# Placing edges by source in one fp16 pass, the basis mix dealt over three stages, slot writes begun earlier

## What is computed

```python
edge_index = jnp.stack([src, dst])
# first layer: a message per edge, summed by source
x_ij = jnp.concatenate([x[src], x[dst]], axis=1)
out = jax.ops.segment_sum(relu(x_ij @ W.T + b), src, num_segments=1250)
# last layer: two relations, 30 bases of 512 x 512 each, for each of two inner layers
w = jnp.einsum('rb,bio->rio', att, basis)
```

## Time and profile before

| what | us |
|---|---|
| median of 3 runs | 1941.36 (1940.92 to 1942.94) |
| span of the profiled execution, first to last instruction | 1934.6 |
| first block of the sort, and loading before it | up to 90.0 |
| second block of the sort | 90.0 to 137.85 |
| bucket stage | 137.85 to 185.06 |
| placing and unpacking | 185.06 to 293.35 |
| counting | 293.35 to 455.20 |

### The profile page before, as it was taken

One profiled execution on the slowest core, in us unless ns is written; L12 is line 12 of the kernel. 1 busy time (PEld: TensorE's weight loads), 2 busy tenths in 40 slices (PEclk: granted clock), 3 DMA queues, 4 the chain that ended last, 5 costly groups with the idle time before them and its releaser, 6 DMA issues. The chain is left out here.

```text
span 1934.6 us, 27686 instructions
## 1 busy us (share of the span) xinstructions
PE 1608.4 (83%) x7565; PEld 981.3 (51%) x7566; DVE 1167.7 (60%) x2310; ACT 471.2 (24%) x884; POOL 705.2 (36%) x605
## 2 busy tenths in 40 slices
PE   6755956776498999998888459998498899999998
PEld 6751633335443555554555435554246545874486
DVE  5779958884365777775467766665774832113222
ACT  4301103432212555554344210000110111001100
POOL 0001877887094776660000347775330010000000
PEclk9997988998698999999899569999799999999999
DMA  0017844005802766682388337776104201430033
GB/s 25 0 47 285 275 136 120 1 1 172 306 27 92 210 197 187 187 169 45 126 317 331 101 100 211 210 209 171 27 1 144 96 1 72 155 122 1 0 136 135
DMA packets 76346, 248.96 MB, mean 129 GB/s; under 512 B 14901, under 2 KB 28582, under 8 KB 68346
## 3 DMA queue, kind: packets, MB, share of 16 engines
q1 hardware_dynamic: 38618, 147.08, 21.1%
q0 software_dynamic: 34592, 96.87, 18.9%
q10 hardware_dynamic: 3072, 4.20, 0.7%
HBM read 215.93 MB, written 32.00 MB: 128 GB/s over the span
## 5 line engine op out<-in xcount | busy, mean ns | idle before, releaser
L664 POOL DMA_INDIRECT tab_slots<-slot_words,slot_address x160 | 238.1, 1488 | 244.5 <-issue 233.3
L693 POOL DMA_INDIRECT e_rows<-tab_h,idx_h x176 | 178.6, 1015 | 293.4 <-POOLq L50 219.8
L1443 PE MATMUL dense_pY<-weights,dense_xT_block 128*128 128x512 f32 x640 | 284.3, 602 | 0.0
L1491 PE MATMUL dense_pY<-parts,dense_number 128*128 128x512 f32 x1000 | 237.7, 399 | 7.1 <-DMA dense_number<-tab_edges_to 7.1
L994 POOL DMA_INDIRECT e_rows<-tab_q,idx_q x192 | 182.0, 948 | 99.4 <-issue 38.9
L1491 PEld LDWEIGHTS dense_pY<-parts,dense_number 128*128 128x128 f32 x1000 | 188.7, 189 | 54.8 <-DMA dense_number<-tab_edges_to 8.6
L787 PE MATMUL e_pS<-e_rows,e_onehot_ring 128*128 128x512 f32 x352 | 194.2, 643 | 22.1 <-DVE e_rows L763 19.2
L1443 PEld LDWEIGHTS dense_pY<-weights,dense_xT_block 128*128 128x128 f32 x640 | 121.9, 194 | 143.1 <-issue 143.1
L1067 PE MATMUL e_pS<-e_rows,e_onehot_f 128*128 128x512 f32 x384 | 181.4, 596 | 0.0
L877 PE MATMUL count_pA<-count_onehot_d,count_onehot_s 128*128 128x512 f16 (+1 forms) x576 | 117.4, 352 | 63.8 <-DVE count_onehot_d L855 60.3
L763 DVE TENSOR_TENSOR e_rows<-e_rows,e_pW 128x1024 f32<-128x1024 f32 x88 | 107.3, 1220 | 69.3 <-DMA e_rows<-tab_h,idx_h 69.0
(11 more groups left out here) (312 smaller groups left out, 2448.4 us busy)
## 6 DMA issues: line engine op xcount, KB each, us to landing
basis_piece<-in_L_gnn_basis_pieces SPq DMA_DIRECT2D x32, 2048.0 KB, 7.9
dense_number<-tab_edges_from SPq DMA_DIRECT2D x20, 1280.0 KB, 5.4
tab_edges_from<-counts_turned SPq DMA_DIRECT2D x10, 1280.0 KB
tab_edges_to<-counts_total SPq DMA_DIRECT2D x10, 640.0 KB
dense_number<-tab_edges_to SPq DMA_DIRECT2D x10, 640.0 KB, 4.6
tab_w<-basis_wout ACTq DMA_DIRECT2D x128, 32.0 KB
weights<-tab_w SPq DMA_DIRECT2D x4, 1024.0 KB, 6.3
weights<-in_L_gnn_W_T SPq DMA_DIRECT2D x3, 1024.0 KB
```

Of the source, the lines that this page charges most:

```text
L664: pool.indirect_dma_start(self.table, bass.IndirectOffsetOnAxis(self.address[:, t:t + 1], 0), self.words[:, t, :], None).then_inc(self.pla ...
L693: pool.indirect_dma_start(self.rows[:, q, s, :], None, self.table, bass.IndirectOffsetOnAxis(self.idx[:, j * 2 + s:j * 2 + s + 1], 0)).the ...
L1443: ins = self.nc.tensor.matmul(self.banks.at(g), self.xt[:, b % 2, c, :], weights[:, c, :], start=c == 0, stop=c == 3)
L1491: ins = self.nc.tensor.matmul(self.banks.at(self.first + b), self.number[:, b % 2, r * NB + k, :], self.parts[r][n][:, k, :], start=k == 0 ...
```

## The change

**Placing.** The packed word goes. For each tile DVE builds `onp` for that tile alone (128 columns) and two `ons` halves of 192 columns, one with the source within its block, one with the target; all three are single-source operations with fp16 input (two iotas, converted once) and fp16 output. PE makes one fp16 matmul of 384 columns per tile. At the end three DVE operations on PSUM write `loc`, `dst` and `idx_q`; the unpacking block is gone. The loops are written out.

**Basis.** The first basis' 16 pieces are dealt 6, 6, 4: six to the sort (two loaded in its first block, the rest and all the mixing in its second), six to the bucket stage as before, four to the placing. Pieces and results lie in the space of `X` and the weights, which are now one tile. The sort's rank lookup is written out for it.

**Slot writes.** 24 in the bucket stage, 36 in placing, 86 in counting, 14 beside storing the counts (before: 0, 56, 88, 16).

```diff
-WITH_BUCKETS = 6
+WITH_SORT, WITH_BUCKETS = 6, 12
...
+    def load_some(self, eng, first, last):
+        if first == 0:
+            eng.dma_start(self.mix[:, :], self.mix_in).then_inc(self.mixed, 16)
+        for n in range(first, last):
+            wait(eng, self.used, (n - 1) * 2)
+            eng.dma_start(self.piece[:, n % 2, :], self.pieces[(n + self.first) * P:(n + self.first + 1) * P, :]
+                          ).then_inc(self.loaded[n % 2], 16)
...
+        basis.allocate(ctx, stage_semaphores(nc, ctx, f"{name}_basis"))
...
+            def _(sp):
+                basis.load_some(sp, 0, 2)
...
+            def _(sp):
+                basis.load_some(sp, 2, basis.steps * 2)
+
+            @block.scalar
+            def _(act):
+                for n in range(basis.steps * 4):
+                    basis.store(act, n // 4, n // 2 % 2, n % 2)
+                basis.end_store(act)
...
+                basis.start_multiply(pe)
+                for n in range(4):
+                    basis.multiply(pe, n // 4, n // 2 % 2, n % 2)
                 pe.wait_ge(prefix_ready, 1)
...
+                for g in range(T // GT):
+                    w = g % 2
+                    wait(pe, taken, g - 1)
+                    for u in range(GT):
+                        t = g * GT + u
+                        ins = nc.tensor.matmul(pg[:, w, u, :, :].rearrange("p n l -> p (n l)"), onehotT[0:HI, t, :],
+                                               pre[:, :, :, t].rearrange("p n l -> p (n l)"), start=True, stop=True)
+                    ins.then_inc(gathered, 1)
+                    if g >= 2:
+                        n = g + 2
+                        basis.multiply(pe, n // 4, n // 2 % 2, n % 2)
...
+        @block.gpsimd
+        def _(pool):
+            table.place(pool, 0, PLACED_WITH_BUCKETS)
...
-            for f, factor in packed:
-                link(nc.vector.scalar_tensor_tensor(value, f, float(factor), value, ALU.mult, ALU.add))
...
+            nc.vector.tensor_copy(iota_p[:, :], C.f("iota_p", EP))
+            nc.vector.tensor_copy(iota_s[:, :], C.f("iota_slot", EP)[:, 0:slots]).then_inc(iota_ready, 1)
+            v.wait_ge(iota_ready, 1)
+            for t in range(T):
+                wait(v, placed, t + 1 - RING)
+                nc.vector.tensor_scalar(onp[:, t % RING, :], iota_p[:, :], pos_p[:, t:t + 1], None, ALU.is_equal)
+                for n in range(2):
+                    ins = nc.vector.tensor_scalar(ons[:, t % RING, n, :], iota_s[:, :], pos_s[:, t:t + 1],
+                                                  values[n][:, t:t + 1], ALU.is_equal, ALU.mult)
+                ins.then_inc(built, 1)
             v.wait_ge(placed, T)
-            nc.vector.tensor_copy(sorted_out, po[:, 0:slots])
+            nc.vector.tensor_scalar(loc, po[:, 0, :], 1.0, None, ALU.subtract)
+            nc.vector.tensor_copy(other, po[:, 1, :])
+            nc.vector.tensor_copy(other_index, po[:, 1, :])
...
+            for t in range(T):
+                pe.wait_ge(built, t + 1)
+                nc.tensor.matmul(po[:, :, :].rearrange("p n s -> p (n s)"), onp[:, t % RING, :],
+                                 ons[:, t % RING, :, :].rearrange("p n s -> p (n s)"),
+                                 start=t == 0, stop=t == T - 1).then_inc(placed, 1)
+                if t == 0:
+                    basis.start_multiply(pe)
+                if t % mixed_after == mixed_after - 1:
+                    n = t // mixed_after
+                    basis.multiply(pe, n // 4, n // 2 % 2, n % 2)
...
-PLACED_WHILE_PLACING, PLACED_WHILE_COUNTING = 56, 144
+PLACED_WITH_BUCKETS, PLACED_WHILE_PLACING, PLACED_WHILE_COUNTING = 24, 60, 146
```

More of the change, by code:

```diff
@@ L173, with __init__, banks, allocate @@
     PIECES = D * D // BCH // BW
-    def __init__(self, nc, name, pieces, mix, wtab, first, last):
+    def __init__(self, nc, name, pieces, mix, wtab, first, last, space=None):
         self.nc, self.name = nc, name
         self.pieces, self.mix_in, self.dst = pieces, mix, wtab
-        self.first, self.steps = first, (last - first) // 2
+        self.first, self.steps, self.space = first, (last - first) // 2, space
     def begin(self, ctx, sem):
+        self.allocate(ctx, sem)
+        self.banks(ctx)
+    def banks(self, ctx):
+        self.ps = ctx.enter_context(self.nc.psum_tensor(f"{self.name}_ps", [P, 4, D], F32))
+    def allocate(self, ctx, sem):
         nc = self.nc
@@ L445, in _, with bucket_edges @@
                                  ).then_inc(summed, 1)
+                basis.start_multiply(pe)
+                for n in range(4):
+                    basis.multiply(pe, n // 4, n // 2 % 2, n % 2)
                 pe.wait_ge(prefix_ready, 1)
[L448 to L462, removed]
+                for g in range(T // GT):
[9 more added lines that the diff above has]
+                        basis.multiply(pe, n // 4, n // 2 % 2, n % 2)
+def bucket_edges(nc, name, C, key, rel, pair_block, tile_bucket, tile_bank, bucket_end, pos_p, pos_s, value, basis,
+                 table):
     with ExitStack() as ctx:
@@ L605, in _ @@
         def _(act):
-            def step(i):
-                for n in range(4):
-                    basis.store(act, i, n // 2, n % 2)
-            peeled(act, basis.steps, step)
+            for n in range(basis.steps * 4):
+                basis.store(act, n // 4, n // 2 % 2, n % 2)
             basis.end_store(act)
@@ L628, in _ @@
             v.wait_ge(placed, T)
-            nc.vector.tensor_copy(sorted_out, po[:, 0:slots])
+            nc.vector.tensor_scalar(loc, po[:, 0, :], 1.0, None, ALU.subtract)
+            nc.vector.tensor_copy(other, po[:, 1, :])
+            nc.vector.tensor_copy(other_index, po[:, 1, :])
         @block.tensor
         def _(pe):
-            def step(i, first=False, last=False):
-                for u in range(STEP):
-                    pe.wait_ge(built, i * STEP + (u + 1))
-                    nc.tensor.matmul(po[:, 0:slots], onp[:, u // TOGETHER % BATCHES, u % TOGETHER, :], ons[:, u % RING, :],
-                                     start=first and u == 0, stop=last and u == STEP - 1).then_inc(placed, 1)
-                    if u % QUARTER == QUARTER - 1:
-                        n = u // QUARTER
-                        if first and n == 0:
-                            basis.start_multiply(pe)
-                        basis.multiply(pe, i, n // 2, n % 2)
@@ L643, in _ @@
-            step(0, first=True)
-            with pe.Fori(1, T // STEP - 1) as i:
-                step(i)
-            step(T // STEP - 1, last=True)
+            for t in range(T):
[8 more added lines that the diff above has]
+                    basis.multiply(pe, n // 4, n // 2 % 2, n % 2)
```

84 lines of the change are left out of this document (35 added, 49 removed).

## The result

The changed kernel takes **1966.35 us** (median of four, 1965.86 to 1970.09) against 1941.14 us: a ratio of 1.0144, 95% interval 1.0127 to 1.0161, so it is 1.4% slower. The forecast was 1956 us, range 1940 to 1976, slower. Sign and range held; the size was 10 us short. Every execution takes 1.7 to 1.9 us more than its span, so the profile of the kernel before (span 1934.6) is of an execution of some 1936.4 us, the fastest of its four; of the 6.8 us that were put down to what lies around the first and the last instruction, 5 are spread between executions. The profile of the changed kernel is of its slowest (1970.09 us, span 1968.2). So the spans differ by 33.6 us where the medians differ by 25.2.

What follows compares the result with a forecast made beforehand. The prediction took POOL's slot writes to bound the placing and DVE the counting. Sort +0.5, bucket stage +8.0, placing +6.2 and counting -0.4 made +14.3 us, hence 1956 us, range 1940 to 1976.

Steps and rivals of the forecast that it cites:

- What bounds the kernel now: Old stages: POOL's 56 slot writes bound the placing, PE and DVE having 15 us to spare; DVE bounds the counting.
- The placing's price: Placing: DVE bounds it at 0.62 us per tile, 114.5 us in all against 108.3, so +6.2 us.
- Break-even: Placing: the cost per tile, 0.53 us, from which rival 1's faster kernel is decided.
- The bucket stage: Bucket stage: POOL's 24 new slot writes wait for DVE's long operations and end the stage, +8.0 us.
- the danger: Bucket stage: the forecast would be wrong if DVE's chain itself grew behind POOL's writes; no size given.
- The sort: Sort's second block: written-out lookups at 1.8 us and mixes at 1.07 us make +0.5 us, between -1 and +6.
- Behind the change: Everything behind the counting: claimed unchanged, 0 us.
- The sum: Whole kernel: +0.5 + 8.0 + 6.2 - 0.4 = +14.3 us, giving 1956 us, slower by 0.7%.
- rival 2: Placing: fp16 one-hots with two scalars don't run at twice fp32, +16.6 us, 1972 us; chance 0.10.
- 1: Placing: per-partition scalars cost nothing, a tile takes 0.33 us and the kernel gets faster, 1909 us; chance 0.14.
- 3: Bucket stage: POOL keeps up and DVE ends the stage, 8 us less, 1948 us; chance 0.15.
- 4: Bucket stage and placing: rival 3, and the placing's writes cost DVE nothing either, 1940 us; chance 0.06.

Runs made afterwards that it cites:

- experiment 4: Kernel before with ten slot writes moved from the placing to the storing of the counts (46, 88, 26): 1926.17 us, ratio 0.9936.
- experiment 5: Changed kernel with the multiplication by the value left out of both one-hot halves: placing 17.6 us shorter; whole time 1975.51 us says nothing, since later gathers read other rows.
- experiment 1: Changed kernel with its 24 slot writes of the bucket stage moved to the placing, which then has 60: 1964.13 us.
- experiment 6: Changed kernel with PE taking the counts' matmuls after the first piece of the basis instead of after the second: 1967.93 us.
- experiment 2: Changed kernel with two basis pieces in the sort instead of six, and eight in the placing instead of four: 1955.18 us.
- experiment 7: Changed kernel, dropped tile allocated again: 1967.97 us; kernel before, placing loops written out: 1947.41 us; experiment 3 with its placing in a loop: 1947.19 us.
- experiment 3: Changed kernel with only the new placing and written-out lookups: no sort mixes, no bucket-stage slot writes, 60 writes in the placing: 1954.81 us.

## Why the prediction was right in sign and short in size

**What bounds the kernel now** held: the earlier trace rows named POOL as the end of the old placing, and experiment 4 took it away for 14 us of that stage.

**The placing's price** held in its make-up. An `onp` lasts 0.24 us (0.236 forecast), an `ons` half 0.317 (0.313). Start to start they are 0.163 and 0.240, where I had 0.156 and 0.233; 0.007 us three times per tile give 0.642 instead of 0.62, and over 160 tiles 3.2 us: the term that was mis-sized. The 36 writes cost 72 x (0.752 - 0.642) = 7.9 us (7.8), the tail from DVE's last one-hot (311.04) to the counting 7.2 us (0.5 + 5.4 + 0.9 = 6.8). The mix in this tail takes 1.94 us, the granted clock being 0.50 there. Break-even lay at 0.53 us per tile; experiment 5 reaches 0.52, without the values.

**The bucket stage** held as to who ends it and by which rows: POOL's waits sum to 14.3 us (15.7 forecast), and the tail is 3.06 us as in the earlier trace rows. The Trainium skill's page "SBUF — State Buffer", section "Who interferes with whom", gives the rule that whoever starts first on the shared port pair keeps it for its whole instruction; the write of 6.48 us beside the scan of 6.82 agrees. DVE's chain grew by 3.3 us, which I had named as the danger. But 2.9 of these are the longer wait for the counts' matmuls, behind a piece that came later and was mixed at the lower clock; experiment 1 doesn't put that down to the writes. And it decided nothing here, because POOL ended 0.87 us later still (experiment 6).

**The sort** was the step that failed. I put the mixes at 1.07 us "the clock being 1.00 in both", and the granted clock fell to 0.50 while PE, with its first mixes and lookups behind it, waited for DVE. Groups of lookups at 1.8 us were right from the third on (1.83); the first two, right behind the mixes, took 2.07 together. Seven mixes at 1.87 from start to start, instead of 1.07, are 5.6 us, and each stands on the path, since PE does lookups and mixes in turn and DVE waits for both. PE's wait of 2.22 us behind the first two groups wasn't in the sum and adds 0.7. At the block's end 2.03 us pass instead of 0.92. Of that I had put 0.5 down to one more clearing, which no row ahead of the change shows; experiment 2, where no store is left at the end, has 1.29 there, 0.37 more. The loads, priced at 1 us, cost 0.22. With +7.03 the stage also left its own bounds (-1 to +6).

**Behind the change** I had written "unchanged". By the runs it wasn't: two pairs of kernels that differ in the placing's loops alone are 8.9 and 7.6 us apart, most of it in the scoring and behind it (experiment 7). The changed kernel itself wasn't run with a loop there.

**The sum.** Against the forecast of 14.3 the touched stages gave 22.8: +6.5 in the sort, -1.6 in the bucket stage, +3.9 in the placing, -0.3 in the counting. By the medians the kernel lost 25 to 29 us, by which runs of the kernel before they are set against; that leaves 2 to 6 us outside these stages, where the two profiles show 10.8. That the time lies inside the range is in part luck: the forecast's own band ended at 1963, and the range went on to 1976 for rival 2, which didn't happen.

**The rivals.** 1 fell with the price per scalar: from start to start an `ons` half takes 0.240 us with two scalars and 0.179 with one (experiment 5: half of 0.521 - 0.163). By the formula of the Trainium skill's page "VectorE: DVE Perf Modes", section "The TRN2 errata — SBUF-src ops pay a fixed extra latency per instruction", it would take an estimated 0.110 us; the trace does not agree. 2 fell: a comparison with a multiplication in fp16 takes 0.317 us where fp32 took 0.368. 3 fell with the five long writes, and 4 with them and with the 0.11 us that a tile loses beside the writes in the placing.

## What to carry to other kernels

Ask first which engine ends a stage: here 14 us of the placing, 11 of the kernel, lay in moving ten small writes, and a new algorithm for the engines that had time to spare gave none. Where short operations are mostly fixed cost, as the one-hots here, count operations and per-partition scalars, not columns or matmul passes. Work put into an engine's waits is free only where the waits are; between the steps of a chain that alternates two engines it is on the path, at whichever clock is granted then.

## What the runs showed of the hardware

- A per-partition scalar operand costs a VectorE operation 58 ns in fp16 (317 against 259 ns), about what the fp32 rows give (59); a second operation with a constant costs 1 ns (252 against 251).
- The granted clock doesn't by itself give the speed of PE's small matmuls: 32 lookups took 2.07 us behind mixes and 3.60 us behind 6.45 us of idling, both at 1.00, and 3.67 us at 0.50 (experiment 2) as well as at 1.00 (experiment 3). What decides is open.
- A slot write that begins while DVE runs a long operation with two inputs in SBUF ends about 1 us behind that operation: 6.48 us beside the scan of 6.82, 3.2 to 3.8 us beside operations of 3.5 to 3.9, in each of the five kernels with 24 writes in the bucket stage. That the writes slow down the loads beside them isn't shown: the first piece was mixed 9.0 to 9.4 us after the stage's start with them and 8.2 to 9.1 without.
- The clock that one mix is granted moves the chain of the bucket stage. Where the counts' matmuls stand behind the second piece, DVE waited 2.6 to 4.0 us for them when that piece was mixed in 1.9 us, and 5.5 to 6.3 when it was mixed in 3.1 to 3.6 (1.00 and 0.55 in experiment 1).
- Loops written out in one stage made a stage some 670 us later slower by 3 and 10 us in the two pairs profiled, though its code was the same; the mechanism wasn't found.
